# A four-layer cross-attention kernel on one Trainium2 core: the loop over groups is turned, so that layer zero and the first keys of the next group stand beside layers one to three of this one

## What is computed

```python
# layer 0: normalised over the last axis, channels as the 64 "rows", softmax over 256 positions
Mn = Wn @ norm(x) + bn;  Mm = Wm @ norm(ctx) + bm;  Ml = Wl @ ctx + bl
x  = Wo @ (Ml @ softmax(Mn.T @ Mm).T) + bo + x
# layers 1 and 2: 16 heads of 16, keys and values from the layer norm of ctx
for l in (1, 2):
    a = layer_norm(ctx) * gamma + beta
    Q, K, V = x @ Wq.T, a @ Wk.T, a @ Wv.T
    x = x + tanh(gate) * (softmax(Q K.T / 4, masked) V) @ Wo.T
# layer 3: one head over all 256 features
q, k, v = x @ w_q.T, ctx @ w_k.T, ctx @ w_v.T
x = x + alpha * (softmax(q k.T / 16) v) @ w_o.T
```

## Time and profile before

| | us |
|---|---|
| median of 3 runs (lowest, highest) | 716.01 (714.12, 716.99) |
| the profiled execution, its own time | 714.7 |
| its span, first to last instruction | 712.5 |
| PE busy | 652.5 (92%) |
| weight loads busy | 578.6 (81%) |
| DVE busy | 494.7 (69%) |
| ACT busy | 463.4 (65%) |
| POOL busy | 203.7 (29%) |
| DMA | 18.18 MB, mean 26 GB/s |

### The profile page before, as it was taken

The page is one execution under the profiler, slowest core; times in us unless marked ns, Lnnn a source line. Parts: engine busy times, 40 slices in busy tenths (PEclk is TensorE's granted clock), DMA queues, the critical chain, the costliest instruction groups (busy, mean ns, idle before and its releaser), DMA issues.

```text
span 712.5 us, 21646 instructions
## 1 busy us (share of the span) xinstructions
PE 652.5 (92%) x8643; PEld 578.6 (81%) x8643; DVE 494.7 (69%) x1083; ACT 463.4 (65%) x893; POOL 203.7 (29%) x169
## 2 busy tenths in 40 slices
PE   2988999989999899989999899998999899998985
PEld 1867898778988799878987789877988789987884
DVE  5857687675777657685776757867577857765575
ACT  1886575865847666665757658486575666676571
POOL 6333610426006250145203370061601533021100
PEclk9999999999999999999999999999999999999999
DMA  6320000200002000200003000020001100000000
GB/s 154 119 63 2 3 2 2 95 2 2 2 31 65 1 2 2 93 4 2 2 2 94 2 2 2 20 77 2 2 2 48 48 2 1 2 33 2 2 2 30
DMA packets 18491, 18.18 MB, mean 26 GB/s; under 512 B 1829, under 2 KB 18341, under 8 KB 18405
## 3 DMA queue, kind: packets, MB, share of 16 engines
q1 hardware_dynamic: 17504, 16.42, 7.3%
q0 software_dynamic: 320, 0.26, 0.4%
q10 hardware_dynamic: 580, 0.14, 0.1%
HBM read 12.63 MB, written 4.19 MB: 24 GB/s over the span
## 4 chain that ended last, share of the span: by engine, by line
PE 45%; issue 26%; POOL 12%; ACT 8%; DVE 4%; DMA 3%; ACTq 1%; SPq 1%; POOLq 0%; DVEq 0%
PE psum L352 7%; PE psum L561 7%; PE psum L354 6%; PE psum L353 5%; PE psum L581 4%; PE psum L634 4%; POOL kbd L1113 3%; ACT work L755 3%; PE psum L437 2%; POOL x_norm L1154 2%; ACT work L741 2%; POOL c_norm L1154 2%; PE psum L627 2%; PE psum L571 1%; ACT v L694 1%
## 5 line engine op out<-in xcount | busy, mean ns | idle before, releaser
L1113 POOL TENSOR_TENSOR kbd<-k_tmp,own_row 128x1024 f32<-128x1024 f32 x32 | 60.6, 1893 | 400.4 <-ACT k_tmp L689 400.4
L922 DVE TENSOR_REDUCE negmax<-psum 128x8 f32<-128x512 f32 x128 | 87.6, 684 | 35.2 <-PE psum L561 35.2
L755 ACT ACTIVATE work<-psum,group_mask 128x512 f32<-128x512 f32 x128 | 80.2, 688 | 28.0 <-PE psum L581 27.8
L926 DVE TENSOR_TENSOR shifted<-psum,negmax 128x512 f32<-128x512 f32 x128 | 88.5, 692 | 8.0 <-ACT work L741 2.9
L741 ACT ACTIVATE work<-shifted 128x512 f32<-128x512 f32 x128 | 77.6, 632 | 13.8 <-DVE shifted L926 13.5
L581 PE MATMUL psum<-const,work 64*128 64x64 f32 x1536 | 67.0, 228 | 17.8 <-ACT work L741 15.6
L581 PEld LDWEIGHTS psum<-const,work 64*128 64x128 f32 x1536 | 55.6, 139 | 32.7 <-issue 29.3
L561 PE MATMUL psum<-kbd,work 64*128 64x128 f32 x1024 | 71.5, 282 | 3.9 <-POOL kbd L1113 2.1
L634 PE MATMUL psum<-v,work 128*64 128x34 f32 x2048 | 69.2, 225 | 5.7 <-ACT work L755 5.7
L634 PEld LDWEIGHTS psum<-v,work 128*64 128x64 f32 x2048 | 64.2, 138 | 12.0 <-issue 10.7
L561 PEld LDWEIGHTS psum<-kbd,work 64*128 64x128 f32 x1024 | 61.7, 188 | 10.7 <-ACT work L706 2.8
(11 more groups left out here) (182 smaller groups left out, 1705.9 us busy)
## 6 DMA issues: line engine op xcount, KB each, us to landing
x_raw<-in_x_dram SPq DMA_DIRECT2D x8, 512.0 KB, 3.9
c_raw<-in_ctx_dram SPq DMA_DIRECT2D x8, 512.0 KB, 4.7
out_dram<-attn SPq DMA_DIRECT2D x16, 256.0 KB, 2.7
mrow_u<-in_mask_dram SPq DMA_DIRECT2D x8, 64.0 KB, 4.6
work<-in_L_xattn_Wq_dram SPq DMA_DIRECT2D x2, 256.0 KB, 4.1
work<-in_L_xattn_Wk_dram SPq DMA_DIRECT2D x2, 256.0 KB, 4.4
work<-in_L_xattn_Wv_dram SPq DMA_DIRECT2D x2, 256.0 KB, 5.0
work<-in_L_xattn_Wo_dram SPq DMA_DIRECT2D x2, 256.0 KB, 6.0
```

Source lines behind the costliest of these rows:

```text
L755: act.activation(probsT[:, slot, :], o[:], ACT.Copy, scale=group_mask[:, i:i + 1]).then_inc(free, 1)
L922: dve.tensor_reduce(negmax[:, i % 2, :], sv, AX_X, ALU.max, negate=True).then_inc(rowmax, 1)
L926: dve.tensor_tensor(shifted[:, i % 2, :].rearrange("t (j k) -> t j k", k=C), sv, negmax[:, i % 2, :].unsqueeze(2).broadcast_to([P, NJ, C]) ...
L1113: pool.tensor_tensor(kbd[l - 1][:, i], k_tmp[:, i, :].rearrange("p (b s) -> p b s", s=C).unsqueeze(2).broadcast_to(each), own_row[:].unsqu ...
```

## The change

The steps of layer 0 (`S X T A` with layer 0) and of `K1` leave the head of the pass and stand at its end, for group g+1; in the last pass they are dropped. The prologue gets the same steps for group 0. The order of all other steps in the pass and in the prologue is written anew (150 entries for the pass). Layer 0 writes a state of its own, `state_in`, which `H`/`L` 0 and 1 and `O1` read; `state` is written from `O1` on. The two units of `probs` and `probsT` are given out in the order in which the transpositions stand (`slot`). Layer 3's exponentials, transposes, `k3T` and `v3` move to the tile `scratch`, whose place in `work` and `k_tmp` layer 0 and `K1` of the next group need. The raw weights of layers 1 and 2 lie in the `kbd` tiles in the prologue. SP loads group g+2 in pass g, once the front steps of group g+1 have read the buffers. On POOL the order becomes `front`, `normalise`, `spread_keys(g, 2)`, `spread_keys` of `K1` for group g+1.

```diff
     def S(l, i):
-        return at("S", l, i)
+        return at("S", l, i) if l or front else []
...
     o = [("SC", 0)]
-    o += S(0, 0) + S(0, 1) + X(0, 0) + X(0, 1) + p("V1", 0) + p("K1", 0) + T(0, 0) + T(0, 1) + S(0, 2) + S(0, 3) + S(0, 4)
...
-    o += p("Q1", 0) + nxt(("ST", 3)) + A(0, 6) + A(0, 7) + S(1, 0) + S(1, 1) + p("V1", 1) + H(1) + copied("V1", 1) + L(1)
-    o += X(1, 0) + S(1, 2) + S(1, 3) + X(1, 1) + T(1, 0) + p("Q1", 1) + p("K2", 1) + X(1, 2) + S(1, 4) + S(1, 5) + X(1, 3)
...
+    o += H(0) + L(0) + p("K2", 0) + p("Q1", 0) + nxt(("ST", 0)) + nxt(("ST", 1)) + p("V1", 0) + S(1, 0) + S(1, 1)
+    o += copied("V1", 0) + H(1) + L(1) + X(1, 0) + S(1, 2) + S(1, 3) + nxt(("ST", 2)) + p("V1", 1) + nxt(("ST", 3)) + X(1, 1)
+    o += p("K3", 0) + p("Q1", 1) + p("K2", 1) + X(1, 2) + X(1, 3) + nxt(("MV", 0)) + T(1, 0) + S(1, 4) + S(1, 5) + S(1, 6)
+    o += S(1, 7) + X(1, 4) + T(1, 1) + X(1, 5) + X(1, 6) + p("V2", 0) + A(1, 0) + A(1, 1) + T(1, 2) + X(1, 7) + p("K3", 1)
+    o += p("AT1", 0) + T(1, 3) + A(1, 2) + p("O1", 0) + H(2) + A(1, 3) + L(2) + f("xT", 0) + p("V3", 0) + p("AT1", 1)
...
+    o += S(2, 3) + X(2, 0) + f("xT", 1) + p("V3", 1) + p("Q2", 1) + X(2, 1) + p("V2", 1) + X(2, 2) + f("V0", 0) + X(2, 3)
+    o += S(2, 4) + S(2, 5) + T(2, 0) + S(2, 6) + S(2, 7) + X(2, 4) + T(2, 1) + X(2, 5) + f("Mn", 0) + A(2, 0) + X(2, 6)
+    o += X(2, 7) + A(2, 1) + T(2, 2) + T(2, 3) + f("Mn", 1) + f("cT", 0) + p("AT2", 0) + A(2, 2) + A(2, 3) + p("O2", 0)
...
+    o += copied("XN", 0) + S(0, 0) + S(0, 1) + S(0, 2) + S(0, 3) + X(0, 0) + p("PV", 0) + f("V0", 1) + copied("PV", 0)
+    o += X(0, 1) + nxt(("E", "V0", 1)) + X(0, 2) + T(3, 1) + X(0, 3) + S(0, 4) + S(0, 5) + T(0, 0) + T(0, 1) + p("PV", 1)
+    o += X(0, 4) + X(0, 5) + T(0, 2) + T(0, 3) + A(0, 0) + A(0, 1) + S(0, 6) + S(0, 7) + X(0, 6) + X(0, 7) + T(0, 4)
+    o += T(0, 5) + A(0, 2) + A(0, 3) + f("K1", 0) + f("K1", 1) + T(0, 6) + T(0, 7) + A(0, 4) + nxt(("E", "K1", 1)) + A(0, 5)
+    o += A(0, 6) + A(0, 7)
...
-            def iteration(g, last):
-                if not last:
-
-                    for i in range(8):
-                        hold(full[i], g * PER[i] + PRO_FILLS[i])
-                    hold(normed, g + 1)
-                    hold(mix_ready, g + 1)
-                    load_group(g + 1)
+            def prefetch(g):
+
+                for f in FRONT[:12]:
+                    bk, n = fill(g, f, False)
+                    hold(full[bk], n)
+                hold(normed, 1 if g is None else g + 2)
+                hold(mix_ready, 1 if g is None else g + 2)
+                load_group(1 if g is None else g + 2)
...
+                    if p % 2:
+                        dve.wait_ge(free, n)
+                        dve.sem_inc(state_ready, 1)
...
+            spread_keys(None, 1, False)
             with pool.Fori(0, NG - 1) as g:
+                front(g)
+                normalise(g)
+                spread_keys(g, 2, False)
                 spread_keys(g, 1, False)
-                front(g)
-                spread_keys(g, 2, False)
-                normalise(g)
-            for l in (1, 2):
-                spread_keys(NG - 1, l, True)
+            spread_keys(NG - 1, 2, True)
```

More of the change, by code:

```diff
@@ L151, in build, with slots_of, slot, ahead @@
     BANK_PRO, NTH_PRO, PRO_FILLS = fills_of(PROLOGUE)
+    def slots_of(order):
+        units = [s for s in order if s[0] == "T" and (s[1] == 0 and s[2] % 2 == 0 or s[1] in (1, 2))]
+        return {(l, i // 2 if l == 0 else i): n % 2 for n, (_, l, i) in enumerate(units)}
+    SLOT, SLOT_LAST, SLOT_PRO = slots_of(ORDER), slots_of(LAST_ORDER), slots_of(PROLOGUE)
+    def slot(g, l, u, last):
+        return (SLOT_PRO if g is None else SLOT_LAST if last else SLOT)[l, u]
+    def ahead(g, per):
+        return 0 if g is None else per * g + per
     def fill(g, step, last, c=0):
@@ L339, in _ @@
             sp.sem_inc(result_free, 1)
-            for i in range(8):
-                sp.wait_ge(full[i], PRO_FILLS[i])
-            with sp.Fori(0, NG - 1) as g:
-                iteration(g, False)
-            iteration(NG - 1, True)
+            hold(x_normed, 1)
+            prefetch(None)
+            with sp.Fori(0, NG - 2) as g:
+                prefetch(g)
+                store(g, False)
+            store(NG - 2, False)
+            store(NG - 1, True)
         @blk.tensor
@@ L410, in proj_step @@
                     used = [("P", "W0" if name == "V0" else "W0T", 0)]
-                o, signal = start_fill(g, step, last, consumed=used, front=fronts("nT") if name in ("K1", "V1") and i == 0 else ())
+                if name == "K1":
+                    used = fronts("nT") + ([("P", "Wk1", 0)] if g is None else [])
+                o, signal = start_fill(g, step, last, consumed=used, front=fronts("nT") if name in ("V1", "K2", "V2") and i == 0 else ())
                 if g is None and i == 0 and name in ("xT", "cT", "V0"):
@@ L717, in state_high @@
             def state_high(g, n, last):
-                bk, nth = fill(g, ("A", 0, 4 * n + 2) if n < 2 else ("P", "O1", n - 2), last)
-                act.wait_ge(freed[bk], released(bk, nth))
+                if n < 2:
+                    act.wait_ge(state_ready, 2 * g + (n + 1))
+                else:
+                    bk, nth = fill(g, ("P", "O1", n - 2), last)
+                    act.wait_ge(freed[bk], released(bk, nth))
                 half = slice(HALF * (n % 2), HALF * (n % 2) + HALF)
-                act.activation(state_hl[0][:], state[:, :, half], ACT.Copy).then_inc(state_hi, 1)
+                act.activation(state_hl[0][:], (state_in if n < 2 else state)[:, :, half], ACT.Copy).then_inc(state_hi, 1)
             def set_mask(g):
```

141 lines of the change are left out of this document (81 added, 60 removed).

## The result

The changed kernel takes 719.35 us (median of 20 runs, 715.34 to 721.97), the kernel before in the same series 715.41 (20 runs, 714.12 to 717.08). The ratio is 1.0048, interval 1.0034 to 1.0062: about half a per cent slower, where 694 us, 3.1% faster, was forecast. The profiled execution took 720.23 us for a span of 718.4; its mean granted clock is 0.973, where it was 0.998 before.

A forecast was written before the change was run, and what follows sets the result against it. PE was taken to bound the kernel, with 4.3 us idle in a pass. 56.2 + 7 × 81.2 + 65.8 = 690.4 us of span, with +2.2 and +1.3 694 us, 3.1% less; own range 687 to 700, 8 in 10 681 to 712.

The forecast's parts named there:

- Waits that come: New waits of PE in a pass, at `Q1`, layer 2 and the tail: +2.1 us, bounds 0.6 to 4.5.
- layer 2: `V0` ahead of the second half of the scores makes PE wait 0.5 us up to `T(2,3)`.
- the tail: End of the pass: ACT has layer 0's exponentials and copies in front of `A(0,2)`, a wait of 0.3 us.
- `Q1` on `state_low` 0: `Q1` waits for `state_low` behind the last `A 0` step: 1.3 us taken, 0.6 to 2.4 possible beside POOL.
- a sign of being right: In the new trace, a wait of 1 us or more ahead of `Q1`, released by a `state_low` of 1.4 or more.
- The POOL queue: Layer 2's keys, spread behind `normalise`, are ready 1.3 us ahead of the first `S 2`; nothing on the sum.
- The rival "slower": POOL's stretched chain makes `S 2` wait 4.4 us in each pass, 85.6 a pass, 725 us in all; chance 0.10.
- Waits that go and seams: In a pass, PE's waits in layers 0, 1 and 3 go, −4.0 us; fewer tiling changes, 39 to 33, −0.6.
- a sign of being wrong: PE's busy time itself, not its idle time, falling by more than the 0.6 us of seams.
- the first rival: Longer distances also take 2 us of hidden waits out of a pass: 79.2 a pass, 680 us; chance 0.12.
- Prologue and last pass: Span up to group 0's `Q1` 56.2 us, ±2; from group 7's `Q1` to the end 65.8, ±1.
- each case for no gain: New waits at their 4.5 us bound (715 us, chance 0.08), or POOL's chain late (725 us, chance 0.10).

The follow-up runs named there:

- after_s48: The changed kernel with only PE's loop head put at slot 48 of a block of 256 instructions; 705.27 us.
- pool_k2_first: The changed kernel with POOL spreading layer 2's keys ahead of the normalisation, PE's loop head where it was; 708.91 us against 720.23.
- after_s128: The changed kernel with only PE's loop head put at slot 128 of a block of 256 instructions; 709.22 us.

## Why the prediction was wrong

**The step that failed is "Waits that come".** It has three terms (`Q1`, layer 2, the tail) and a sum of 2.1 us. It has no term for the jump back, and the one for POOL beside a `state_low` it puts on the wrong `state_low`. What came in a pass with a jump was more, and from other places:

| term of a pass | forecast | measured |
|---|---|---|
| standstill at the jump back | none | +3.2 (19.4 in six) |
| low clock behind it | none | +1.3 |
| `Q2` on `state_low` 2 | none | +1.5 |
| `Q1` on `state_low` 0 | 1.3 | 0, inside the standstill; 0.8 without one |

By these, 81.2 + 3.2 + 1.3 + 1.5 − 1.3 = 85.9, the mean measured; and for the interval that ends without a jump 81.2 + 1.3 + 1.5 − 1.3 + 0.8 = 83.5, against 83.22 (the low clock at its start belongs to the jump before it). after_s48 is the check from the other side: with neither standstill nor low clock in its five middle passes, 81.2 + 1.5 − 1.3 + 0.8 = 82.2, and 82.2 is what they take (its first and last take 83.4 and 83.5). With 4.7 more in six intervals, 2.0 in one, and 0.6 and 1.6 less in prologue and end, the 690.4 us of the sum become the 718.4 of the span.

- **The jump back** had no term at all. I compared the lists and took the turn of the loop for free because the earlier trace rows show no wait there. It was free in the kernel before only by its place. The head's slot, with nothing else changed, moves the time by 20 us, and the rows of the branch and of the 16 KB packets show that the standstill is a wait for instructions: 3.1 to 3.5 us in the branch, which ends 2.3 to 2.9 us after a packet starts. The row was there before the change too, with 0.4 us a jump.
- **`state_low` beside POOL.** The mechanism was in the text, with its rule, the Trainium skill (SBUF — State Buffer, SBUF: two separate sides): a DVE instruction with two SBUF inputs and a GpSimd one keep each other out. I applied it to `state_low` 0, and looked for POOL's effect otherwise only in `S 2`. `state_low` 0 was short after all, 0.69 us in seven of eight groups and 1.34 in one, where 1.4 or more was a sign of being right; without a standstill ahead of it PE waited 0.8 us for it, against 0.5 to 0.6 reckoned for a short one. The moved spreads of layer 2 run in the very microseconds of `state_low` 2: 3.25 us instead of 0.69. With one more POOL instruction to wait for, as I had it, 0.69 + 1.89 = 2.6 would be the worst; it waited for two. pool_k2_first shows the cause and its price, 10.5 us of waits in seven passes, 1.5 each.
- **The POOL queue** was otherwise right: the second spread ends at 341.95, before `S 2`, which waits for nothing. The rival "slower" by POOL's chain did not happen; that it came out slower is no credit to it.
- **Waits that go and seams**: the waits named did go, and with both causes away a pass is 81.0 us against 81.2. That the sum fits so well is in part luck. 1.1 us of a pass are standstill, which covers the 1.3 forecast for `Q1`. Within the rest two errors cancel: PE's busy time is 77.77 us, 1.9 less than in the earlier trace rows, not 0.6, which was a sign of being wrong; and the visible waits other than "issue" are 1.9 us a pass, not 0.8. The 1.3 of busy time beyond the seams may be the hidden waits of the first rival; no run separates them from dearer seams.
- **Layer 2** was forecast to wait 0.5 us ahead of `T(2,3)`; it waits 0.5; layer 0 at the tail waits 0.5 instead of 0.3. **Prologue and last pass**: 55.6 and 64.2, the first within its ±2, the second 0.6 beyond its ±1.
- The range ended at 712, since each case for no gain was a mechanism of data and queues. A term for the loop's own machinery, for which the earlier trace rows give no bound, would have had to widen it.

**Still open.** What starts a packet, and so why it starts ahead of the branch in one place and behind it in another; that it starts when PE comes into the block that holds the branch fits the slots, but no run isolates it. Why the entry's branch is dear at 0, 48 and 64 and cheap at the others. A slot between 0 and 48, or a way to have the last pass's code brought too, wasn't tried. In which slot the head of the kernels before and after lies is not known from the traces.

## What to carry to other kernels

Whoever changes what stands ahead of a long loop on PE moves the loop's head and its jump, and that alone was worth 3% in one kernel here (701 to 721 us) and nearly 5% in the other (715 to 749); compare two versions at fixed slots, or try several of each, before you judge the edit. A wait on "issue" at the first instruction of the body is the sign of it, the duration of the branch on the loop's own line is the measure (0.4 us where it was harmless, 3.2 where not), and a lower granted clock behind it is the second half of the bill. When an instruction of POOL moves, look at every DVE instruction with two SBUF inputs in the stretch that it moves into, not only at those who need its result.

## What was not expected of the hardware

- One jump back of PE costs between nothing visible and 3.5 us by the place of the loop in blocks of 256 instructions, in a loop whose jump is marked as likely. At 64 it is worst; at 48 it is nothing, but entering and leaving then cost 5.0 together, so that 192 has the best sum of those tried.
- 3.2 us without a matmul are enough for the granted clock to be 0.62 over the 4.4 us that follow (1.3 us lost); after 0.94 us it stays at 1.00. In after_s128 it stays at 1.00 behind the standstills of 1.35 and 1.70 us and falls to 0.61 and 0.64 over 4.4 us behind two of 2.67 and 2.63.
- A `state_low` of 0.69 us took 3.25 us beside two POOL instructions one after the other (3.75 us together), and ended only after the second.
- The profile does show instructions being brought: 16 KB packets of a queue of their own. The time from the start of one to the end of the branch that waits for it was 2.3 to 2.9 us, in 68 cases.
